# Layer 0's edge features of a two-layer graph network: one load, a copy inside SBUF, and a low part across partitions

## What is computed

```python
# layer 0: src, dst are the edges' ends, dst is sorted
msg  = relu(x[src] + edge_attr_64 @ W_e + b_e)            # 21250 x 512
aggr = segment_sum(msg, dst, num_segments=1250)
h    = (1 + eps) * x + aggr
h    = silu(bn(h @ W1 + b1)); h = silu(bn(h @ W2 + b2)); x1 = layernorm(x + h)
# layer 1: the same pattern with edge_attr_128, then a GRU cell and a norm
```

## Time and profile before

| | us |
|---|---|
| median of 3 runs | 839.12 |
| fastest and slowest of the 3 | 836.28, 842.1 |
| span of the profiled execution | 836.8 |
| layer 0's edges, from the span's start to the first dense product | 235.69 |
| TensorE, VectorE, ScalarE, GpSimd busy | 781.1, 636.8, 449.6, 362.0 |

### The profile page before, as it was taken

One profiled execution on the slowest core, in us unless ns is written; L12 is line 12 of the kernel. 1 busy time (PEld: TensorE's weight loads), 2 busy tenths in 40 slices (PEclk: granted clock), 3 DMA queues, 4 the chain that ended last, 5 costly groups with the idle time before them and its releaser, 6 DMA issues.

```text
span 836.8 us, 11419 instructions
## 1 busy us (share of the span) xinstructions
PE 781.1 (93%) x3734; PEld 628.3 (75%) x3734; DVE 636.8 (76%) x1126; ACT 449.6 (54%) x809; POOL 362.0 (43%) x381
## 2 busy tenths in 40 slices
PE   7898999888999999798699999999999999999995
PEld 5565666555689999686477777788777798989895
DVE  7788899989989816387699999999984372626255
ACT  4887899888854413211467777778762121111122
POOL 6777777777500000023777777777720000000011
PEclk9999999999999999899799999999999999999998
DMA  8999988888620050014688888888830210200011
GB/s 229 314 304 303 275 259 264 255 249 252 181 98 1 8 195 0 1 51 159 203 261 295 252 259 256 260 255 256 255 115 4 76 76 1 76 1 1 1 51 72
DMA packets 49389, 134.38 MB, mean 161 GB/s; under 512 B 8265, under 2 KB 8521, under 8 KB 48944
## 3 DMA queue, kind: packets, MB, share of 16 engines
q0 software_dynamic: 26720, 87.58, 35.1%
q1 hardware_dynamic: 22116, 45.59, 16.7%
q10 hardware_dynamic: 492, 0.45, 0.2%
HBM read 128.47 MB, written 5.12 MB: 160 GB/s over the span
## 4 chain that ended last, share of the span: by engine, by line
PE 61%; DMA 11%; POOL 10%; DVE 8%; issue 6%; ACT 3%; SPq 0%; DVEq 0%; POOLq 0%; ACTq 0%
PE banks L518 39%; PE banks L545 11%; POOL raw L448 9%; DMA raw<-in_x,src_sb 6%; PE banks L575 4%; PE banks L576 3%; DVE msg_lo L1114 3%; DMA raw<-table_dram,src_sb 2%; DVE raw L1122 2%; DMA x_in<-in_x 2%; PE banks L573 1%; PE banks L598 1%; ACT banks L853 1%; PE banks L589 1%; DVE stats L1251 1%
## 5 line engine op out<-in xcount | busy, mean ns | idle before, releaser
L448 POOL DMA_INDIRECT raw<-in_x,src_sb x167 | 169.7, 1016 | 52.5 <-issue 44.5
L448 POOL DMA_INDIRECT raw<-table_dram,src_sb x167 | 164.2, 983 | 59.8 <-issue 38.4
L470 POOL TENSOR_TENSOR moments<-moments,minus_half 128x1 f32<-128x1 f32 x32 | 20.3, 635 | 302.3 <-DVE moments L1257 302.3
L853 ACT ACTIVATE banks<-raw 128x512 f32<-128x512 f32 x166 | 99.1, 598 | 79.7 <-DMA raw<-table_dram,src_sb 52.6
L1122 DVE TENSOR_TENSOR raw<-banks,raw 128x512 f32<-128x512 f32 x168 | 114.4, 681 | 20.3 <-PE banks L545 15.8
L1114 DVE SCALAR_TENSOR_TENSOR msg_lo<-raw,msg_hi 128x512 fp32r<-128x512 f32 x168 | 114.1, 679 | 4.5 <-ACT msg_hi L897 3.8
L575 PE MATMUL banks<-msg_hi,hot 128*128 128x512 f32 x293 | 115.9, 396 | 0.7 <-DVE agg L1137 0.4
L576 PE MATMUL banks<-msg_lo,hot 128*128 128x512 f32 x293 | 114.9, 392 | 0.0
L897 ACT ACTIVATE msg_hi<-raw 128x512 fp32r<-128x512 f32 x168 | 104.3, 621 | 14.4 <-DVE raw L1122 13.9
L545 PE MATMUL banks<-We_hi,attr 97*128 97x512 f32 x167 | 87.7, 525 | 16.5 <-ACT banks L853 15.1
L1114 DVE SCALAR_TENSOR_TENSOR msg_lo<-banks,msg_hi 128x512 fp32r<-128x512 f32 x125 | 84.8, 678 | 2.1 <-ACT msg_hi L897 1.8
(11 more groups left out here) (170 smaller groups left out, 1725.1 us busy)
## 6 DMA issues: line engine op xcount, KB each, us to landing
attr_sb<-in_attr SPq DMA_DIRECT2D x84, 128.0 KB, 4.6
attr_sb<-in_attr SPq DMA_DIRECT2D x42, 256.0 KB, 3.8
Wg_raw<-in_Wg SPq DMA_DIRECT2D x3, 1536.0 KB, 6.3
raw<-in_x,src_sb POOLq DMA_INDIRECT x167, 4.8
raw<-table_dram,src_sb POOLq DMA_INDIRECT x167, 4.1
x_in<-in_x SPq DMA_DIRECT2D x5, 512.0 KB, 14.3
rows<-in_x SPq DMA_DIRECT2D x1, 2560.0 KB, 12.2
table_dram<-table_sb SPq DMA_DIRECT2D x9, 256.0 KB, 2.0
```

What stands on the lines that cost most here:

```text
L448: pool.indirect_dma_start(rows_of(L, t), None, tables[L], bass.IndirectOffsetOnAxis(ap=src_sb[:, t:t + 1], axis=0)).then_inc(gathered[t % ...
L470: nc.gpsimd.tensor_tensor(moments[:, slot * 4 + 2:slot * 4 + 3], moments[:, slot * 4 + 1:slot * 4 + 2], minus_half[:, 0:1], ALU.pow).then_ ...
L853: return nc.scalar.activation(to, of, ACT.Copy)
```

## The change

In layer 0 SyncE loads the features once, to partitions 0 to 63. ScalarE rounds them once, into `attr_hl` on partitions 0 to 63, and one step earlier than before (even steps, chunk (j+4)/2). A DMA from SBUF to SBUF on SyncE's queue copies this high part to `attr_1`. VectorE reads raw and high features on partitions 0 to 63 and writes the difference to partitions 64 to 127. TensorE waits for the copy as well at each chunk's first tile. Layer 1 is as before.

```diff
--- before.py
+++ after.py
@@ -257,6 +257,7 @@
              "window_added", "attr_high", "attr_split"))
         placed, primed = ([sem(f"{n}{L}") for L in range(2)] for n in ("placed", "primed"))
         gathered = [sem(f"gathered{i}") for i in range(RAW)]
+        attr_copied = [sem(f"attr_copied{i}") for i in range(RING)]
         attr_in = [[sem(f"attr_in{L}_{i}") for i in range(RING)] for L in range(2)]
 
         lf_free, lf_idx_ready, lf_gathered, lf_attr_in, lf_mm, lf_msg_steps, lf_hot_ready, lf_summed, lf_copied, lf_turned, lf_added = (
@@ -333,10 +334,13 @@
                 parts = attr_parts[L]
 
                 wait(sp, attr_split[L], c - RING + 1)
-                for h in range(P // parts):
-                    sp.dma_start(attr[L][h * parts:(h + 1) * parts, c % RING, :],
-                                 attr_dram[L][:, c * CHUNK * P:(c + 1) * CHUNK * P]
-                                 ).then_inc(attr_in[L][c % RING], 16)
+                sp.dma_start(attr[L][0:parts, c % RING, :], attr_dram[L][:, c * CHUNK * P:(c + 1) * CHUNK * P]
+                             ).then_inc(attr_in[L][c % RING], 16)
+
+            def copy_high_features(c):
+
+                sp.wait_ge(attr_high[0], c + 1)
+                sp.dma_start(attr_1[0:ED0, c % RING, :].bitcast(F32), attr_hl[0:ED0, c % RING, :].bitcast(F32)).then_inc(attr_copied[c % RING], 16)
 
             def load_leftover_attr(L):
 
@@ -355,8 +359,11 @@
             for c in range(RING):
                 load_chunk(0, c)
 
+            copy_high_features(0)
+
             sp.wait_ge(add_mm[0], 1)
             for c in range(RING, CHUNKS):
+                copy_high_features(c - 2)
                 load_chunk(0, c)
                 q = c - RING
                 if q < XQ:
@@ -364,6 +371,8 @@
                 k = c - 3 * RING
                 if 0 <= k < KD:
                     sp.dma_start(W1_raw[:, k, :], W1[k * P:(k + 1) * P, :]).then_inc(w1_in, 16)
+            for c in range(CHUNKS - 2, CHUNKS):
+                copy_high_features(c)
             load_leftover_attr(0)
 
             sp.wait_ge(agg_start, BLOCKS)
@@ -439,7 +448,7 @@
                     wait_table(1)
                 elif t == 2:
 
-                    pool.wait_ge(attr_in[0][0], 32)
+                    pool.wait_ge(attr_in[0][0], 16)
 
                 if t >= RAW and odd(t):
                     pool.wait_ge(placed[L], (t - RAW) // 2 + 1)
@@ -529,6 +538,8 @@
                 i, c, ks = t // 2, t // CHUNK, slice(t % CHUNK * P, (t % CHUNK + 1) * P)
                 if t % CHUNK == 0:
                     pe.wait_ge(attr_split[L], c + 1)
+                    if L == 0:
+                        pe.wait_ge(attr_copied[c % RING], (c // RING + 1) * 16)
                 if odd(t):
 
                     pe.wait_ge(placed[L], i + 1)
@@ -862,13 +873,12 @@
 
             def high_features(L, c):
 
-                act.wait_ge(attr_in[L][c % RING], (c // RING + 1) * (32, 16)[L])
+                act.wait_ge(attr_in[L][c % RING], (c // RING + 1) * 16)
                 if c >= RING:
 
                     act.wait_ge(add_mm[L], chunk_done(c - RING))
-                copy((attr_hl, attr_hi)[L][:, c % RING, :], attr[L][:, c % RING, :]).then_inc(attr_high[L], 1)
-                if L == 0:
-                    copy(attr_1[0:ED0, c % RING, :], attr[0][0:ED0, c % RING, :]).then_inc(attr_high[0], 1)
+                parts = attr_parts[L]
+                copy((attr_hl, attr_hi)[L][0:parts, c % RING, :], attr[L][0:parts, c % RING, :]).then_inc(attr_high[L], 1)
 
             def place(L, t):
 
@@ -923,8 +933,10 @@
                     if L == 0 and 0 <= j - TURN_X < BLOCKS:
                         start_sums(j - TURN_X)
 
-                    if odd(j) and 2 <= (j + 3) // 2 < CHUNKS:
-                        high_features(L, (j + 3) // 2)
+                    if L == 0 and not odd(j) and (j + 4) // 2 < CHUNKS:
+                        high_features(0, (j + 4) // 2)
+                    if L == 1 and odd(j) and 2 <= (j + 3) // 2 < CHUNKS:
+                        high_features(1, (j + 3) // 2)
                     for g in range(GROUPS):
                         if last_step(g) + SUM_LAG + COPY_AFTER == j:
                             copy_window(L, g)
@@ -1089,10 +1101,10 @@
 
             def low_features(L, c):
 
-                dve.wait_ge(attr_high[L], (c + 1) * (2, 1)[L])
+                dve.wait_ge(attr_high[L], c + 1)
                 s = c % RING
                 if L == 0:
-                    i = low_part(attr_hl[ED0:P, s, :], attr[0][ED0:P, s, :], attr_hl[ED0:P, s, :])
+                    i = low_part(attr_hl[ED0:P, s, :], attr[0][0:ED0, s, :], attr_hl[0:ED0, s, :])
                 else:
                     i = low_part(attr_lo[:, s, :], attr[1][:, s, :], attr_hi[:, s, :])
                 i.then_inc(attr_split[L], 1)
```

## The result

Over 20 runs each the kernel before took 839.6 us (median) and the changed kernel 844.65 us; the ratio of the two on record is 1.0048, with a 95% interval of 1.0033 to 1.0062. That is 0.0048 x 839.6 = 4.0 us slower (the medians lie 5.05 us apart): within the 1% that was forecast as "no change", but more than the 0.7 us of the sum, and well apart from zero. One execution of each (882.57 us before; 1429.3 us after, at a granted clock of 0.834) fell in a slower state of the chip and is not in the ratio. The profiled execution spans 842.8 us, where the earlier trace rows has 836.8.

What follows compares the result with a forecast made beforehand. Layer 0's edge stage was taken as bound by GpSimd's back-to-back issue of 167 gathers. Tail -0.3 and late copies +1.0 gave +0.7 us on 836.8, 837.5 profiled, about 839.8 us with 2.3 added; range 834.5 to 846.

Steps and rivals of the forecast that it cites:

- rival A: Layer 0: the copy chain becomes the bound from a landing of 5.9 us on; +12 to +37 us, 851 to 876; chance 0.11.
- ScalarE's 25.9 us, worth nothing: Layer 0: 42 second copies of 617 ns go from ScalarE; nothing queues for this time, so directly worth 0.
- The -0.3 us for the tail: Layer 0's tail: one ScalarE copy less ahead of the last messages, 0 to -0.5 us, taken as -0.3.
- VectorE's low part at the same price: Layer 0: reading partitions 0 to 63 and writing 64 to 127 keeps 690 ns; worth 0 even at twice that.
- The wait at chunk 1, 3 us and free: Layer 0's start: copy 1 goes out at 14.6 us, TensorE stands about 3 us; 0 for the end.
- Landing in calm stretches 4.2 us: Layer 0's calm part: the copy lands like half-chunk loads, in 4.2 us, which fits the 4.4 us left.
- Landing in the full stretch 6 to 8 us: Layer 0, transfer engines full: copies land in 6 to 8 us, each some 1 to 3 us late.
- The loop and the 5.9 us from which lateness adds up: Layer 0: two chunks need 4.6 us plus landing L, gathers 10.5; above L = 5.9 us TensorE falls behind.
- the term of +1.0 us: Layer 0: late copies hold GpSimd 0 to 3 us beyond the 2.4 us free, limiting itself; taken as +1.0.
- a sentence on the second load: Layer 0: replacing the load by a copy keeps 84 issues of 128 KB and the bytes moved; no term in the sum.
- Rival B: Layer 0: fewer HBM bytes relieve the full stretch and shorten gathers; -4.5 us, 834.6, at most -13; chance 0.07.
- Rival C: Layer 0: copies land like the 2.0 us store, no lateness anywhere, only the tail; 838.8 us; chance 0.22.

Runs made afterwards that it cites:

- the one-load kernel: Kernel before with one load for two, ScalarE rounding twice in the old slot, VectorE reading across partitions, no DMA copy: 839.37 us, ratio 0.9987.
- the old-slot kernel: Changed kernel with ScalarE's high part back on odd steps, one step later, so each copy goes out later: 847.39 us, ratio 1.0086.
- the copy that ended on partitions 64 to 127: Changed kernel with the full copy sent where TensorE doesn't read or wait, ScalarE making the second high part: 840.33 us, ratio 1.0018.
- the kernel with the early slot: Kernel before with one load, ScalarE rounding twice one step earlier, VectorE reading across partitions, no DMA copy: 836.73 us, ratio 0.9954.

## Why the prediction was right, and where it was off

*The forecast and the range* were right: within 1%, inside 834.5 to 846. The size was off: +0.7 us in the sum, +4.0 us measured. The median of 844.65 lies above the 838.5 to 842 that was given for the forecast's own mechanism, and inside the whole range only by the part up to 846 that was kept for the lower end of rival A, which did not come: so far the range was right by luck.

*ScalarE's 25.9 us, worth nothing*: right. Its busy time on the page fell from 449.6 to 430.3 us, by 19.3 and not by the 26 of the signs: 0.46 us for each of the 42 copies, which is near the 0.5 us start to start that the prediction has for one. No gather starts earlier for it. The -0.3 us for the tail did not come: from the last gather's start to the dense part it is 11.2 us before and 12.0 after, in the mean of three traces each.

*VectorE's low part at the same price*: right, 686 for 690 ns, here and in the one-load kernel.

*The wait at chunk 1, 3 us and free*: right as far as it shows. 3.5, 2.0 and 3.0 us in three traces, and the kernel without it gained nothing that can be told from zero.

*Landing in calm stretches 4.2 us*: right, 4.4. *Landing in the full stretch 6 to 8 us*: too low for 20 to 60 us, where the three traces have 9.4, 8.6 and 8.4 us, near the upper end that was kept for the range; at 60 to 100 us it was 7.2, 6.6 and 6.5. The nearest row was a load of half a chunk at 72 to 78 us, and for 20 to 60 us the top of the earlier trace rows should have been taken. Before, the half loads landed in 7.4 us from 20 to 60 (median of 14; 8.8 and 7.1 in the other two traces), and in the traces of the changed kernel the loads landed there in 8.6, 9.1 and 9.0, so the copy is no faster for staying inside SBUF:

```profile
attr_sb<-in_attr SPq DMA_DIRECT2D x14, 128.0 KB, 7.4
```

*The loop and the 5.9 us from which lateness adds up*: right in kind. The holds come before 62 us, where L is above 5.9, and after 100 us GpSimd waits no longer than 0.3 us for any slot. By the loop two chunks would need 4.6 + 9.4 = 14.0 us against 10.5, so three rounds make 10.5 us of lateness; what arrived at GpSimd was 2.4 to 3.8 us. That it limits itself was in the text, and the old-slot kernel shows it: later copies, a held GpSimd, landing down from 9.4 to 6.4 us. The mark of 219 to 223 us from first to last gather held (222.3, 221.0 and 219.3), but its "no wait over 0.3 us" was a wrong mark, and it did not fit with the term of +1.0 us either, which needs such waits: they are 1.8 to 2.8 us long, 3.0 us held in the mean for the 1.0 taken.

*The step that failed* is a sentence on the second load: that issues stay 84 "and the bytes that the engines move stay the same", from which the exchange of a load for a copy was put at no change and no price. The sentence is true and the conclusion was the wrong one to draw. One load less with the early rounding gave 3.9 us, and a full copy takes 5.4 us back even where TensorE doesn't wait for it. Together that is 1.5 us of loss (ratio 1.0018, by its interval 0.2 to 2.9 us) where the sum has nothing. The 3.9 us are of both edits: one load less with the late rounding gave 0.13%, which can't be told from zero, and the early rounding with two loads was not run. The rest is the term for the wait, 1.0 us in the sum: 2.5 us by the ratios, but only with the traffic, which also sets the landing time that the wait then sees. GpSimd was held 3.0 us in the mean for this term's 1.0, and the 2.5 us, good to some 2 us, agrees with that.

*Rival A* (the chain as the bound, +12 us and more) did not come: landing is 4.4 us in the calm part, below 5.9. The rule weighed, of partitions 0 to 63 reached by half the ports, "SBUF — State Buffer", "Door 1: The DMA port swizzle", of the Trainium skill, asks 3.6 us a chunk as an estimate from that page; the copy's 4.4 us in the calm part stand beside 4.7 us for the loads of the same trace, so a bound by it does not show. But the copy that ended on partitions 64 to 127 landed in 3.5 us there, so a smaller cost of both ends on one half is open. *Rival B* (relief): the relief of one load less exists, 0.46% in the kernel with the early slot, but not by B's mechanism. B tied the gathers' excess over 0.94 us to the load of the transfer engines. In the one-load kernel with late rounding that load at 60 to 100 us is 0.84 and a gather takes 1029 ns; before, with 1.03, it takes 1016; and with the same load, 0.85, the kernel with early rounding has 992. The excess goes with something else, told in the last section. The highest rate was misread too: the 313 GB/s of the earlier trace rows are a mean over 40 us, in which the same trace has slices of 1 us with up to 393. *Rival C* (no lateness anywhere, copies landing like the 2.0 us store) did not come: they landed in 4.4 us at the calmest.

*What stays open.* Layer 0 accounts for 1.2 of the 3.2 us between the mean spans; 1.9 us lie between the layers, where no instruction is changed. A store that landed 1.7 us later in two of three traces and moments at which TensorE's granted clock falls (in the first trace of after it was 0.50 from 393 to 396 us, the 1.2 GHz level, with products of 0.63 us for 0.39) are candidates; three traces of each don't settle it. Nor is it settled why the one-load kernel gains 0.33% from the early slot; shorter gathers may be a part (992 for 1029 ns in the two traces: 167 x 0.037 = 6.2 us less, though the second is of an execution 3 us over its median), the reason for which is argued below and was not tried by an edit. And why the copy lands sooner from ScalarE's queue was not tested.

## What to carry to other kernels

A transfer that replaces another of the same size is two terms, and each is to be priced at the stretch where the transfer engines are full: here dropping a load and rounding a step earlier gave 0.46%, and the copy inside SBUF took 0.64%. What a wait on a transfer costs depends on the transfer's landing under that load, so traffic and wait are to be thought of together; with a quarter of the bytes the same wait showed no cost. Where an engine has time to spare, as ScalarE here with nearly half its time idle, let it repeat a cheap rounding rather than ask the full transfer engines for a copy: that kernel, at 836.73 us, beat both.

## What the runs showed of the hardware

*GpSimd's issue of a gather becomes longer when it begins beside a VectorE instruction that reads two tiles from SBUF.* In the kernel before, at 49.78 us, it begins beside the add, one of whose inputs comes from the product's bank, and takes 0.95 us; at 51.04 beside the low part of the features and at 52.62 beside the even tile's low message, both of which read only SBUF, it takes 1.28 and 1.26.

```profile
49.48 0.69 DVE L1122 TENSOR_TENSOR raw<-banks,raw 128x512 f32<-128x512 f32 x1 [0.82 <-PE banks L545]
49.78 0.95 POOL L448 DMA_INDIRECT raw<-in_x,src_sb  x1 [0.30 <-issue]
...
50.80 0.69 DVE L1037 TENSOR_TENSOR attr_hl<-attr_sb,attr_hl 64x512 fp32r<-64x512 f32 x1
...
51.04 1.28 POOL L448 DMA_INDIRECT raw<-in_x,src_sb  x1 [0.30 <-DVE msg_lo L1114]
...
52.37 0.68 DVE L1114 SCALAR_TENSOR_TENSOR msg_lo<-raw,msg_hi 128x512 fp32r<-128x512 f32 x1
...
52.62 1.26 POOL L448 DMA_INDIRECT raw<-in_x,src_sb  x1 [0.30 <-issue]
```

Counted over layer 0 in the traces of all kernels here, 308 gathers took over 1.15 us. Some 285 of them began inside such an instruction (low message of an even tile, one-hot, low features), the rest inside another or one of the setup or at such an instruction's edge, and none inside the add or an odd tile's low message, which have one input in a bank, although 40% of all gathers began there (32 to 51% by kernel). Not each overlap makes it longer. In sum it is 7 to 14 us a kernel above the undisturbed 0.945 us (7.3 in the third trace of after, 8.1 in the fastest kernel, 12.1 before, 13.9 in the one-load kernel with late rounding), by how GpSimd's beat of 1.25 to 1.6 us falls on VectorE's. This is a count over traces, not an edit that took one thing away; but it holds without exception for the add. The Trainium skill, "SBUF — State Buffer", section "Who interferes with whom", says that a VectorE instruction with two SBUF inputs contends with a GpSimd instruction that reads SBUF; these traces agree, with the indirect gather's issue as that instruction, lengthened by about 0.3 us. The same section infers that a `tensor_tensor` leaves the generation of descriptors alone; if the gather's issue is counted as that, these traces do not agree, and the measurement decides.

*A copy of 128 KB inside SBUF costs the transfer engines about as much as a load of that size from HBM.* With one load a chunk their share at 60 to 100 us was 0.85; with the copy added it was 1.00 (nobody waiting) and 1.03 to 1.04 (the changed kernel), and with two loads and no copy 0.99 to 1.04. The copy landed in 4.4 us calm and 8.4 to 9.4 us at its fullest, where half loads had 3.8 to 4.2 calm and 7.1 to 8.8 full. The bytes read from HBM fell with the change from 128.47 to 122.97 MB, and the time did not.
